# Layer norm of x worked out for four batches at once in every second group, with x loaded by four batches

## The reference

```python
def _layernorm(x, axis=-1, eps=1e-05):
    m = jnp.mean(x, axis=axis, keepdims=True)
    v = jnp.var(x, axis=axis, keepdims=True)
    return (x - m) / jnp.sqrt(v + eps)
...
x = x + jnp.tanh(g_xattn[0]) * _L0_xattn_ref(_layernorm(x, axis=-1), ctx_768, mask, Wq, Wk, Wv, Wo)
x = x + jnp.tanh(g_ffn[0]) * _L0_ffn_ref(_layernorm(x, axis=-1), W1, b1, W2, b2)
```

## Time and profile before

| | |
|---|---|
| runs | 1670.09, 1671.91, 1670.24 us |
| profiled execution | 1668.12 us, its span 1666.3 us |
| busy in the span | PE 1511.3 (91%), PEld 1010.6 (61%), DVE 1487.7 (89%), ACT 938.2 (56%), POOL 668.6 (40%) |
| mean granted TensorE clock | 0.98 of full speed |
| x loads | 64 of 256 KB, 2.7 us from issue to landing |

### The profile page before, as it was taken

One profiled execution on the slowest core, in us unless ns is written; L12 is line 12 of the kernel. 1 busy time (PEld: TensorE's weight loads), 2 busy tenths in 40 slices (PEclk: granted clock), 3 DMA queues, 4 the chain that ended last, 5 costly groups with the idle time before them and its releaser, 6 DMA issues.

```text
span 1666.3 us, 48258 instructions
## 1 busy us (share of the span) xinstructions
PE 1511.3 (91%) x14501; PEld 1010.6 (61%) x14501; DVE 1487.7 (89%) x4375; ACT 938.2 (56%) x1799; POOL 668.6 (40%) x813
## 2 busy tenths in 40 slices
PE   3899999999999999999999999997999999999998
PEld 2566666666666666666666666664666666666665
DVE  7799999999999999999999999987888888888886
ACT  2465656565656666566656565644555554555554
POOL 5355555455554545554555555452111111111111
PEclk9799999999999999999999999986999999999999
DMA  2333333333333333333333333311010110101101
GB/s 79 89 97 85 94 85 86 97 86 97 83 96 83 97 84 93 87 89 92 86 97 83 98 81 97 80 47 55 27 38 25 38 36 27 38 25 38 38 25 51
DMA packets 207471, 117.93 MB, mean 71 GB/s; under 512 B 24912, under 2 KB 207184, under 8 KB 207440
## 3 DMA queue, kind: packets, MB, share of 16 engines
q1 hardware_dynamic: 207440, 117.54, 26.1%
HBM read 32.53 MB, written 16.78 MB: 30 GB/s over the span
## 4 chain that ended last, share of the span: by engine, by line
PE 54%; DVE 26%; issue 13%; ACT 4%; DVEq 2%; DMA 0%; ACTq 0%
PE bank L1060 12%; PE bank L308 9%; PE bank L1090 5%; PE bank L1089 5%; DVE smax L745 5%; PE bank L332 4%; PE bank L315 4%; PE bank L299 4%; DVE xres L790 3%; DVE rstd L685 3%; DVE k L715 2%; DVE rstd L687 2%; PE bank L387 2%; DVE y L1047 2%; DVE rstd L678 2%
## 5 line engine op out<-in xcount | busy, mean ns | idle before, releaser
L915 POOL TENSOR_TENSOR probl<-prob 128x512 f16<-128x512 f32 x512 | 528.9, 1041 | 535.8 <-ACT prob L597 534.9
L597 ACT ACTIVATE prob<-bank,masks 128x512 f32<-128x512 f32 x512 | 345.2, 687 | 144.9 <-PE bank L367 144.9
L745 DVE TENSOR_REDUCE smax<-bank 128x4 f32<-128x512 f32 x512 | 348.1, 681 | 14.5 <-PE bank L332 10.6
L1076 DVE TENSOR_TENSOR hidl<-hid 128x512 f16<-128x512 f32 x256 | 226.9, 886 | 79.5 <-ACT hid L1071 78.8
L1071 ACT ACTIVATE hid<-bank,b_sb 128x512 f32<-128x512 f32 x256 | 175.9, 687 | 212.3 <-PE bank L1060 206.1
L1060 PE MATMUL bank<-y,w1T 128*128 128x512 f16 x1024 | 262.9, 379 | 29.9 <-DVE y L1047 28.4
L1154 POOL TENSOR_TENSOR xres<-xres,b2g 128x1024 f32 (+1 forms) x32 | 75.7, 2365 | 431.3 <-ACT yln L1024 413.4
L1089 PE MATMUL bank<-w2T,hid 128*128 128x256 f16 x1024 | 237.4, 273 | 1.4 <-ACT w2T L1004 1.4
L1090 PE MATMUL bank<-w2T,hidl 128*128 128x256 f16 x1024 | 237.3, 273 | 0.0
L332 PE MATMUL bank<-k_rows,q_rows 34*128 34x128 f16 x2048 | 228.0, 222 | 6.8 <-DMA q_rows<-smaxT 3.4
L367 PE MATMUL bank<-q_rows,k_rows 50*128 50x128 f16 x2048 | 204.4, 221 | 0.9 <-DMA q_rows<-smaxT 0.9
(11 more groups left out here) (90 smaller groups left out, 2555.7 us busy)
## 6 DMA issues: line engine op xcount, KB each, us to landing
q_rows<-q SPq DMA_DIRECT2D x512, 64.0 KB, 2.6
k_rows<-k SPq DMA_DIRECT2D x512, 64.0 KB, 2.5
xres<-in_x_dram SPq DMA_DIRECT2D x64, 256.0 KB, 2.7
out_dram<-ystage SPq DMA_DIRECT2D x32, 512.0 KB, 2.9
ctx_sb<-in_ctx_dram SPq DMA_DIRECT2D x64, 192.0 KB, 3.1
q_rows<-smaxT SPq DMA_DIRECT2D x128, 8.0 KB
w_raw<-in_L_ffn_W_dram SPq DMA_DIRECT2D x2, 1024.0 KB, 6.7
prob<-in_L_xattn_Wq_dram SPq DMA_DIRECT2D x1, 256.0 KB, 3.9
```

Source lines behind the costliest of these rows:

```text
L597: act.activation(prob[u][:], st_bank[u % 2][:], ACT.Exp, bias=0.0, scale=masks[g.parity][:, 2 + b:3 + b]).then_inc(exp_done, 1)
L745: dve.tensor_reduce(smax[:, b, u * UH:(u + 1) * UH], sm_bank[u % 2][:].rearrange("p (h j) -> p h j", h=UH), AX.X, ALU.max).then_inc(max_ta ...
L915: pool.tensor_tensor(probl[u][:], prob[u][:], prob[u][:].bitcast(BF16)[:, 1::2], ALU.subtract).then_inc(prob_split, 1)
```

## The change

Layer norm of x is worked out for four batches (a half) at a time, and x is loaded four batches at a time (512 KB). The 14 parts all stand in the even group of the loop's pair, for the half two ahead, with part 0 as the first thing that VectorE does in the group; an odd group has none. Scale and shift of the four batches get a tile of their own, `norm`, which only parts 12 and 13 write; so the wait for `ln_done` moves from part 3 to part 12. The step -(variance + eps)/2 moves from part 3 to part 2. ScalarE's `apply_x` of the two groups of a half reads the two halves of `norm`. SP's load waits for `ln_ready` and stands in the odd group's part alone. In the prologue the norms are those of half 0 and half 1; the load of x for half 2 is issued before the loop, and `over_groups(sp, sp_group, 3)` leaves the last six groups of SP unrolled instead of four. In the last group `norm_y` runs its parts 0 to 13 in this new order, and its wait for `y_done` is at part 12 too.

```diff
@@ rows and semaphores
-        rstd = sb("rstd", [P, 4, QB], F32)
+        rstd = sb("rstd", [P, 3, QB], F32)
+        norm = sb("norm", [P, 2, QB], F32)
...
-        def load_x(sp, g):
-            sp.dma_start(xres[:, bass.ds(g.batch(0), 2), :], x_v[:, bass.ds(g.batch(0), 2), :]).then_inc(
-                x_in[g.parity], 16)
+        def load_x(sp, half):
+            sp.dma_start(xres[:, bass.ds(half * QB, QB), :], x_v[:, bass.ds(half * QB, QB), :]).then_inc(x_in, 16)
...
-            x_past = held(2 * (g.n + 3))
-            if left >= 4:
-                sp.wait_ge(ln_done, x_past)
-                load_x(sp, g.after(4))
+            x_past = held(g.half + 3) if g.parity == 1 else None
+            if g.parity == 1 and left >= 6:
+                sp.wait_ge(ln_ready, x_past)
+                load_x(sp, g.half + 3)
@@ apply_x
-            act.wait_ge(ln_ready, g.n + 1)
+            act.wait_ge(ln_ready, g.half + 1)
@@ ln_part
             elif i == 2:
-                last = dve.tensor_scalar(t, meanvar[:, 0:n, 1], EPS, None, ALU.add)
+                dve.tensor_scalar(half, meanvar[:, :, 1], EPS, -0.5, ALU.add, ALU.mult)
+                last = dve.tensor_scalar(t, meanvar[:, :, 1], EPS, None, ALU.add)
...
-                last = dve.scalar_tensor_tensor(y, t, 1.5, y, ALU.add, ALU.mult)
+                last = dve.scalar_tensor_tensor(norm[:, 0, :] if i == LN_PARTS - 2 else y, t, 1.5, y, ALU.add,
+                                                ALU.mult)
@@ norm_x
+        def norm_x(dve, half, parts):
             for i in parts:
                 if i == 0:
-                    dve.wait_ge(x_in[g.parity], 16 * (g.half + 1))
-                if i == 3 and not (isinstance(g.half, int) and g.n == 0):
-                    dve.wait_ge(ln_done, 2 * g.n)
+                    dve.wait_ge(x_in, 16 * (half + 1))
+                if i == LN_PARTS - 2 and not (isinstance(half, int) and half == 0):
+                    dve.wait_ge(ln_done, QB * half)
@@ dve_first
-            norm_x(dve, g1, range(LN_PARTS))
             low_q(dve, g0)
...
-            norm_x(dve, g0.after(2), range(0, LN_AHEAD))
+            norm_x(dve, 1, range(0, LN_PARTS - 2))
             low_v(dve, g0)
-            norm_x(dve, g0.after(2), range(LN_AHEAD, LN_PARTS))
+            norm_x(dve, 1, range(LN_PARTS - 2, LN_PARTS))
...
-            norm_x(dve, g0.after(3), range(0, LN_AHEAD))
@@ dve_group
-                if i < LN_AHEAD and left >= 4:
-                    norm_x(dve, g4, (i,))
-                if i >= LN_AHEAD and left >= 3:
-                    norm_x(dve, g3, (i,))
+                if g.parity == 0 and left >= 4:
+                    norm_x(dve, g.half + 2, (i,))
+            norm(0)
             take_max(dve, g, 1, 2)
-            norm(8)
             if not first:
                 add_attention(dve, g.batch(0) - 2)
-            norm(9)
+            norm(1)
             take_max(dve, g, 1, 3)
             round_max(dve, g, 1)
-            norm(10)
+            norm(2)
             low_max(dve, g, 1)
+            norm(3)
             if not first:
                 read_weighed(dve, g.batch(0) - 1, 1, 1)
                 normalise(dve, g.batch(0) - 1, 1, 1)
-            norm(11)
             if left >= 2:
                 low_q(dve, g2)
-            norm(12)
+            norm(4)
             if left >= 1:
                 take_max(dve, g1, 0, 0)
-            norm(13)
+            norm(5)
             if left >= 1:
                 take_max(dve, g1, 0, 1)
+            norm(6)
             read_weighed(dve, g.batch(0), 0, 0)
+            norm(7)
             normalise(dve, g.batch(0), 0, 0)
             if left >= 1:
                 take_max(dve, g1, 0, 2)
             if left >= 2:
                 low_k(dve, g2)
+            norm(8)
             if not first:
                 add_attention(dve, g.batch(0) - 1)
+            norm(9)
             if left >= 1:
                 take_max(dve, g1, 0, 3)
                 round_max(dve, g1, 0)
                 low_max(dve, g1, 0)
-            norm(0)
+            norm(10)
             read_weighed(dve, g.batch(0), 0, 1)
-            norm(1)
+            norm(11)
             normalise(dve, g.batch(0), 0, 1)
-            norm(2)
             if left >= 1:
                 take_max(dve, g1, 1, 0)
-            norm(3)
+            norm(12)
             if left >= 1:
                 take_max(dve, g1, 1, 1)
-            norm(4)
+            norm(13)
             read_weighed(dve, g.batch(1), 1, 0)
-            norm(5)
             normalise(dve, g.batch(1), 1, 0)
-            norm(6)
             if left >= 1:
                 low_v(dve, g1)
-            norm(7)
```

More of the change, by code:

```diff
@@ L19 @@
 LN_PARTS = 5 + 3 * NEWTON
-LN_AHEAD = 8
 class Group:
@@ L169, in bass_gated_cross_attention_ternary_ffn @@
         gates_set = sem("gates_set")
-        x_in = [sem(f"x_in{p}") for p in range(2)]
+        x_in = sem("x_in")
         ctx_loaded = [sem(f"ctx_loaded{p}") for p in range(2)]
@@ L531, in apply_x @@
             for b in range(2):
-                act.activation(xln[:, b, :], row_of(g.batch(b)), ACT.Identity, bias=rstd[:, 3, b:b + 1],
-                               scale=rstd[:, 1, b:b + 1]).then_inc(ln_done, 1)
+                r = 2 * g.parity + b
+                act.activation(xln[:, b, :], row_of(g.batch(b)), ACT.Identity, bias=norm[:, 1, r:r + 1],
+                               scale=norm[:, 0, r:r + 1]).then_inc(ln_done, 1)
         def copy_xT(act, g):
@@ L658, in ln_part @@
         def ln_part(dve, i, rows, step, base, ready):
-            n = len(rows)
-            half, y, t, shift = (rstd[:, k, 0:n] for k in range(4))
+            half, y, t = (rstd[:, k, :] for k in range(3))
             if i > 0:
@@ L670, in ln_part @@
             elif i == 1:
-                dve.tensor_copy(t, stats[:, 0:n, 1])
-                for b in range(n):
+                dve.tensor_copy(t, stats[:, :, 1])
+                for b in range(QB):
                     last = dve.bn_aggr(meanvar[:, b, :], stats[:, b, :])
             elif i == 2:
-                last = dve.tensor_scalar(t, meanvar[:, 0:n, 1], EPS, None, ALU.add)
+                dve.tensor_scalar(half, meanvar[:, :, 1], EPS, -0.5, ALU.add, ALU.mult)
+                last = dve.tensor_scalar(t, meanvar[:, :, 1], EPS, None, ALU.add)
             elif i == 3:
-                dve.tensor_scalar(y.bitcast(I32), t.bitcast(I32), -0.5, RSQRT_SEED, ALU.mult, ALU.add)
-                last = dve.tensor_scalar(half, t, -0.5, None, ALU.mult)
+                last = dve.tensor_scalar(y.bitcast(I32), t.bitcast(I32), -0.5, RSQRT_SEED, ALU.mult, ALU.add)
             elif i == LN_PARTS - 1:
-                dve.scalar_tensor_tensor(shift, meanvar[:, 0:n, 0], -1.0, y, ALU.mult,
+                dve.scalar_tensor_tensor(norm[:, 1, :], meanvar[:, :, 0], -1.0, norm[:, 0, :], ALU.mult,
                                          ALU.mult).then_inc(ready, 1)
@@ L693, in row_of @@
             return xres[:, bass.ds(batch, 1), :].rearrange("p o d -> p (o d)")
-        def norm_x(dve, g, parts):
+        def norm_x(dve, half, parts):
             for i in parts:
                 if i == 0:
-                    dve.wait_ge(x_in[g.parity], 16 * (g.half + 1))
-                if i == 3 and not (isinstance(g.half, int) and g.n == 0):
-                    dve.wait_ge(ln_done, 2 * g.n)
-                rows = [row_of(g.batch(b)) for b in range(2)] if i == 0 else (None,) * 2
-                ln_part(dve, i, rows, ln_step, g.n * (LN_PARTS - 1), ln_ready)
+                    dve.wait_ge(x_in, 16 * (half + 1))
+                if i == LN_PARTS - 2 and not (isinstance(half, int) and half == 0):
+                    dve.wait_ge(ln_done, QB * half)
+                rows = [row_of(half * QB + b) for b in range(QB)] if i == 0 else ()
+                ln_part(dve, i, rows, ln_step, half * (LN_PARTS - 1), ln_ready)
         def low_q(dve, g):
@@ L796, in dve_first @@
             g0, g1 = Group(0, 0), Group(0, 1)
-            norm_x(dve, g0, range(LN_PARTS))
+            norm_x(dve, 0, range(LN_PARTS))
             dve.wait_ge(mask_transposed, 1)
@@ L1011, in norm_y @@
             for i in parts:
-                if i == 3 and not (isinstance(g.half, int) and g.n == 0):
-                    dve.wait_ge(y_done, QB * g.n)
-                rows = [row_of(g.n * QB + b) for b in range(QB)] if i == 0 else (None,) * QB
+                if i == LN_PARTS - 2:
+                    if isinstance(g.half, int) and g.n == 0:
+                        dve.wait_ge(ln_done, B)
+                    else:
+                        dve.wait_ge(y_done, QB * g.n)
+                rows = [row_of(g.n * QB + b) for b in range(QB)] if i == 0 else ()
                 ln_part(dve, i, rows, y_step, g.n * (LN_PARTS - 1), y_ready)
@@ L1023, in apply_y @@
             for b in batches:
[L1024 to L1025 removed]
+                act.activation(yln[:, b, :], row_of(g.n * QB + b), ACT.Identity, bias=norm[:, 1, b:b + 1],
```

(9 more changed lines are left out.)

13 lines of the change are left out of this document (5 added, 8 removed).

## The result

The changed kernel takes 1719.09 us (median of 4 runs, 1707.83 to 1735.87) beside 1670.16 us for the kernel before (4 runs, 1667.74 to 1671.91): ratio 1.0271, 95% interval 1.0215 to 1.0328, slower. (The ratio leaves out the run of 1735.87, a slow one, over 1.5% above the fastest; the other three have a median of 1715.76.) The prediction was 1662, range 1638 to 1680. The profiled execution took 1722.41 (span 1720.6).

What follows compares the result with a forecast made beforehand. TensorE and VectorE were taken to bound the kernel together, handing work to each other. 29 x (0.77 - 1.15), 28 x 0.12, -1.1 and +0.45 summed to -8.3 us, giving 1662, range 1638 to 1680.

Steps and rivals of the forecast that it cites:

- Odd start: Before the odd group's context transposes: no layer norm stands there any more, TensorE's idle goes, -1.15 us in 29 groups.
- Even start: Four bn_stats between low_v and take_max replace held operations: idle 1.10 stays and grows, +0.12 us in 28 groups.
- Middle: Even group's middle: part 8 waits for a GpSimd subtraction, delaying the addition and TensorE's xln transposes, +0.77 us in 29 groups.
- The walk: Stepping through VectorE's operations in the even group from 601.10, pricing each by the GpSimd work running where it lands.
- The rest of the even group: Parts 10, 12 and a normalise held 0.3, 0.4, 0.6 us, 9, 11, 13 hardly; low_v covered by 1.05 us.
- rival A: Slower: the cover ahead of low_v in the even group fails, +25 us, 1695; chance 0.20.
- Loads ... Cost 0: SP's x load waits for part 13; moves queued behind it land before the rough scores near 626, cost 0.
- Prologue: Before low_v(0), twelve parts on four batches take 4.1 us instead of 2.45, against an idle of 1.22: +0.45 us.
- D: All removed VectorE operations count until TensorE alone sets the pace: 2.4 us a pair, 70 in all, 1600; chance 0.05.

Runs made afterwards that it cites:

- experiment 1: The changed kernel with SP's x load waiting on ln_step for part 0 instead of ln_ready (part 13): 1739.07 us, ratio 1.0413.
- Experiment 6: The kernel before plus two unused VectorE reductions of 384 columns ahead of the second addition of even groups: 1744.68 us, ratio 1.045.
- experiment 4: The changed kernel with GpSimd's subtraction cut to 8 of 512 columns and a memset filling the rest: 1635.08 us, ratio 0.9799.
- 5: Four batches, SP waiting on ln_step, but the parts at the places of the kernel before (0 to 7 even, 8 to 13 odd group): 1633.38 us.
- 8: The kernel of experiment 1 with parts 8 and 9 moved behind the low maxima and 10 to 13 one place later: 1626.38 us, ratio 0.9737.
- 7: The kernel before plus two unused VectorE reductions ahead of the first take_max of even groups: 1690.76 us, ratio 1.0127.
- Experiment 9: The changed kernel with only the part places of 8, SP waiting on ln_ready (part 13) again: 1672.93 us, ratio 1.0021.
- Experiment 11: The kernel before, still two batches per norm, with parts 7, 8 and 9 moved out of the low_v-to-addition chain: 1619.31 us, ratio 0.9708.
- 2: The changed kernel with part 8 behind the second addition and part 9 behind the take_max after it: 1761.30 us, ratio 1.055.
- 3: The changed kernel with the edits of experiment 1 and 2 together: 1764.43 us, ratio 1.0582.
- experiment 10: The kernel of 8 with the next norm's four bn_stats moved to the odd group, in two pairs: 1614.66 us, ratio 0.967.

## Why the prediction was wrong

- **Odd start (-1.15 x 29): right.** Line 287 starts without idle in every odd group of the loop.
- **Even start (+0.12 x 28; idle 1.1 to 1.3): right**, 1.16 (+0.06, half of what I had). Group 60's idle went too.
- **Middle (+0.77 x 29, part 8 held to the subtraction's end, idle about 0.9): right in mechanism and size**: part 8 from 640.03 to 640.88, line 277 idle 0.89 instead of 0.16. The walk stopped there. The rounding, 0.8 us later than before, also came under a subtraction: the 0.33 at line 345. The group of 16.62 holds it.
- **"The rest of the even group": "parts 9, 11 and 13 hardly" held: wrong.** Part 11 took 1.01 us, part 13 0.77, while part 12, for which I had 0.4, took 0.15. Low_v still came in time, so rival A (its cover fails) didn't happen.
- **"Loads ... Cost 0": the step that failed first.** I had part 13 set `ln_ready` some 4.2 us before the odd start; it was held and ended 2.8 before it. And I had looked at the rough scores that read the moved rows, 8 us away, and not at the last item of SP's queue for the same group, the move of the maxima, whose reader comes sooner (5.85 us behind the odd start). It costs about 1.0 us in 19 odd groups (17.85 beside 16.81 to 16.87 in experiment 1), about 20 us; in the other ten TensorE was late anyway.
- **No term for TensorE's clock: the step that failed by most.** I priced 0.77 us of idle at 0.77 us. In ten even groups it cost 4.0 to 4.4 us more. Experiment 6 makes the same idle in the kernel before and gets the same stretches; 4, 5 and 8 take the idle in the middle away and the stretches go; 7, with 1.64 us at the start, gets five short ones.
- **Prologue (+0.45): neither shown nor refuted; +6.1 us up to group 2.** 4.3 of it come before group 0, and not from the change: TensorE's first rise to 2.4 GHz stands at 47.3 us in this record and at 27.6 in that of before (eight matmuls of line 307 took 4.64 us, beside 2.58), and experiments 8 and 9, whose prologues are the same, show one of each (46.9 and 28.0; group 0 starts at 56.30 and 52.11). The other 1.8 us, between the starts of groups 0 and 2, are unexplained.
- **D and its rule.** The Trainium skill, "VectorE: DVE Perf Modes", § Rules for kernel authors, says to minimise the number of operations. Experiment 11 speaks against taking that as the measure here: 0 operations fewer, 48.8 us gained.

By my own steps with the measured even group and the odd group that follows it in experiment 1 (16.62 + 16.87 instead of 33.92, x 29 = -12.5, and -1.1) the time would have been about 1657, inside the forecast's own range. What was missed is on top. For the profiled execution: 1668.1 - 13.6, + 20 for SP's wait, + 43 for the clock, + 5.5 for prologue and end, make 1723; it took 1722.4.

**Open.** Why only some groups fall. The changed kernel and experiment 1 have the same idles in the same even groups, and 10 and 21 stretches. Where stretches follow each other their starts lie 37.5 us apart, one pair with a stretch. Experiment 9 has idles of 0.8 and 0.56 in the middle of odd groups, 4.3 us apart, and three stretches; in the changed kernel and in 6 the two idles are 1.6 us apart. That this distance matters is a guess, and 2 and 3 speak against it: there it is 0.15 and 0.86 us, and the falls are the most frequent. The one fall of experiment 10 has hardly any idle before it, so idle isn't the whole account.

## What to carry to other kernels

Where an in-order queue gets a later wait, walk everything behind it to its reader, to the last item of the same round: the one that hurts may not be the one beside the wait. An idle of one microsecond of TensorE amid short matmuls isn't priced by its length alone; read the granted clock behind it, and try to keep it out of the middle of a stage, even if it must come back at the start (76.6 and 22.7 us here). Small VectorE operations with two SBUF inputs go where nothing on the critical chain stands behind them, and their places are worth trying before their number: three moved lines gained nearly what the best rewrite did.

## What the runs showed of the hardware

- **The hold.** A VectorE operation of 0.15 us with two SBUF inputs took up to 1.02 under a GpSimd subtraction that reads SBUF; line 684's mean was 492 ns, and 159 (0.18 us at most) where GpSimd mostly wrote. The Trainium skill states this in "SBUF — State Buffer", § Who interferes with whom; experiment 4 agrees.
- **One input can be enough.** The rounding (line 752, a tensor_scalar on 16 columns of SBUF) took 0.68 at 641.97 under a subtraction, and in experiment 4 0.61 at 596.80, to 597.41, under a memset that ran from 596.87 to 597.39. My walk left it out, though the trace of before shows the like: the copy of part 1, with one SBUF input, at 611.31, took 0.98 and ended at 612.29, where the pair of subtractions that began at 610.21 (2.05 together) ends. The same section names tensor_scalar and copy among the operations that can take the shared pair in a 2-port mode; the rows agree.
- **The clock.** TensorE fell from 2.4 to 1.2 GHz at 354.54, after idles of 0.89 and 0.33 us; it had been busy 9.51 of the 11.00 us before. It was busy without a gap in the 10 us that followed, with 67 matmuls beside 109 in the 11 us before, and the clock stayed down until 364.8.
- **The clock at the beginning** rises to 2.4 GHz in one of two places, at 27.6 to 29.5 or at 46.6 to 47.3 us in the 13 traces, in kernels with the same prologue too; the start of group 0 moved with it from 52.11 to 56.30.
